# Attention units of a macaron layer: four places per unit in the projection stream in place of three, and two loads of the output projection issued earlier

## The chip, the cores and the metric

The kernel runs on all 8 NeuronCores of one Trainium2 chip. Every core works on its own rows, with no exchange between cores. The metric is the device time of the slowest core in microseconds.

## What is computed

The input has shape (4, 4096, 2048), in float32. One layer applies three residual blocks, each behind a layer norm: a feed-forward block, attention, and the same feed-forward block again.

```python
x = x + 0.5 * ffn(layernorm(x))      # relu(x W1) -> 8 softmax weights; V, U of rank 64 per weight
x = x + attn(layernorm(x))
x = x + 0.5 * ffn(layernorm(x))

# attn: 16 heads of 128; blocks of 64 tokens see the blocks at a distance of at most 2
mask = where(abs(block_i - block_j) <= 2, 0, -1e30)
scores = q @ k.T * 128 ** -0.5 + mask
out = softmax(scores) @ v            # per head, then out @ Wo
```

## The kernel before

A core computes 2048 rows of one batch entry (16 tiles of 128) and reads one tile more (17, `NT`) for the keys and values at its edge. All matmuls take bf16 operands. The program is written engine by engine: `Prog` keeps a list of instructions for each engine, `op` makes each VectorE and ScalarE instruction wait for the one before it on its own engine, and nothing is reordered later. What a helper issues first stands first in the engine's queue.

The kernel has four stages: the first feed-forward block, attention, the output projection with Wo, and the last feed-forward block. The changed lines are in the second and third.

**Attention.** The outer loop runs over 8 pairs of heads (`pr`), the inner one over 6 groups of tiles (`GROUPS`: 3, 2, 3, 3, 3, 3 tiles). For each group `proj` issues *pieces*: K for each head of the pair, Q for each head, and V for each tile. A piece is 16 matmuls into one of the four banks `R[0..3]`. K and Q pieces have as many columns as the group (384, or 256 for two tiles; the last group's Q pieces have 256, since the 17th tile has no queries), V pieces 256. ScalarE evicts K (line 675) and V (line 663), VectorE evicts Q (line 680). A pair has 41 pieces.

**Units.** A *unit* is the attention of one query tile for the two heads of a pair; a pair has 16, so there are 128. `unit` returns closures:

- `scores` (lines 763 to 780): four matmuls into the single PSUM tile `pS`, the maximum over keys on VectorE (line 770), two exponentials on ScalarE into `Praw[b]` (line 773), the reciprocal of the sums on VectorE (line 778), and two multiplications into `Pn[b]` on VectorE (line 780).
- `turn` (lines 786 to 799): six transposes of `Pn[b]` on TensorE (line 791) into the single tile `pL`, and one copy to `PTs[b]` on VectorE (line 799).
- `values` (lines 801 to 822): six PV matmuls (line 806) from `PTs[b]` into `R[4]`, a copy to `ost` on VectorE (line 814), and after a group's last unit a store of `ost` to the DRAM tensor `od` on SP's queue.

`b` alternates between two buffers. After every piece `between` issues what has been planned for this slot, in the order in which it was planned. `start_unit(k, ...)` plans `scores` at slot k, `turn` at k+3 and `values` at k+4. `next_units` starts the units that a finished group makes possible, two slots apart, from the slot after the next group's first piece; a group gives 2 or 3 units. So the units of one group run between the pieces of the next, and those of the last group between the next pair's first pieces, or, after the last pair, between the first pieces of the output projection.

**Output projection.** `wo_piece(t, cg)` issues 16 matmuls of 512 columns (line 923) for a tile and a quarter of the columns, from `Ob[g % 2]` (attention's output for a group, read back from `od`) and `Wo[cg]`; VectorE adds the result to the residual tile `Xc` (line 929). The first twelve pieces are those of tiles 0 to 2, and the last units run between them. `load_o(g)` and `load_x1(t)` are issued on SP's queue. For groups 0 and 1 they are issued once the pair loop has ended. `Ob` lies in the memory of one of the two K, V and Q buffers, which the last pair doesn't use. `load_o(2)` is issued when the pieces of tiles 0 to 2 are done. `load_w1c(0)` on POOL's queue waits for the last PV and the last stores of `ost` (`attn_end`).

Of the kernel before, what the change touches and what calls it, by code (L numbers as in the profile page):

```python
# [19 lines left out]
NQ = 16  # L20
# [6 lines left out]
QGROUPS = [(0, 3), (3, 2), (5, 3), (8, 3), (11, 3), (14, 2)]  # L27
NG = 6
GROUP_OF = {t: g for g, (a, n) in enumerate(GROUPS) for t in range(a, a + n)}
PAIRS = 8  # L30
# [111 lines left out]
def build_nc():  # L142
# [31 lines left out]
    def S(name):  # L174
        if name not in sems:
            sems[name] = Sem(ctx.enter_context(nc.semaphore(name)))
        return sems[name]
# [3 lines left out]
    def view(t, off, *dims):  # L181
        return bass.AP(t, off, [[t.ap().ap[0][0], 128], *[list(d) for d in dims]])
# [71 lines left out]
    def w_cols(dram, col0, width):  # L254
        n = dram.shape[1]
        return bass.AP(dram, col0, [[n, 128], [128 * n, 16], [1, width]])
# [487 lines left out]
    def unit(pr, t):  # L744
        s = pr % 2
        u = units[0]
        units[0] += 1
        b = u % 2
        j0 = 1 if t == 0 else 0
        c0 = j0 * 128  # L750
        w = 384 - c0
        g_k = GROUP_OF[t + 1]
        kept = {}

        def scores():
            p.wait("tensor", *[kq_end[(pr, g)] for g in range(g_k + 1)], q_end[(pr, GROUP_OF[t])],
                   S_ended[0])
            for h in range(2):
                for half in range(2):
                    lo = max(c0, 64 * half)  # L760
                    hi = 320 + 64 * half
                    key = (t - 1) * 128 + lo
                    tok = p.mm(lambda e, h=h, half=half, lo=lo, hi=hi, key=key: e.matmul(  # L763
                        pS[64 * half:64 * half + 64, h * 512 + lo: h * 512 + hi],
                        Qb[s][:, h * NQ * 128 + t * 128 + 64 * half:
                              h * NQ * 128 + t * 128 + 64 * half + 64],
                        Kb[s][:, h * NT * 128 + key: h * NT * 128 + key + hi - lo],
                        start=True, stop=True), last=(h == 1 and half == 1))
            a = att[b]
            mx = p.op("vector", lambda e: e.reduce_max(  # L770
                a[:, 0:2], view(pS, c0, (512, 2), (1, w)), AX.X, negate=True), tok)
            for h in range(2):
                ex = p.op("scalar", lambda e, h=h: e.activation(  # L773
                    Praw[b][:, h * 384 + c0:(h + 1) * 384],
                    pS[:, h * 512 + c0: h * 512 + 384], AF.Exp, bias=a[:, h:h + 1],
                    accum_out=a[:, 2 + h:3 + h]), mx, pn_free[b])
            S_ended[0] = ex
            p.op("vector", lambda e: e.reciprocal(a[:, 4:6], a[:, 2:4]), ex)  # L778
            for h in range(2):
                nm = p.op("vector", lambda e, h=h: e.tensor_scalar_mul(  # L780
                    Pn[b][:, h * 384 + c0:(h + 1) * 384],
                    Praw[b][:, h * 384 + c0:(h + 1) * 384], a[:, 4 + h:5 + h]),
                    kept.get("pt"))
            kept["nm"] = nm

        def turn():
            p.wait("tensor", kept["nm"], PT_ended[0])
            for h in range(2):
                for j in range(j0, 3):
                    o = h * 384 + j * 128  # L790
                    tok = p.mm(lambda e, o=o: e.transpose(  # L791
                        pPT[:, o:o + 128], Pn[b][:, o:o + 128], idb[:, :]),
                        last=(h == 1 and j == 2))
            pn_free[b] = tok
            if j0:
                out, src = (view(x, 128, (384, 2), (1, 256)) for x in (PTs[b], pPT))
            else:
                out, src = PTs[b][:, :], pPT[:, 0:768]
            PT_ended[0] = kept["pt"] = p.op("vector", lambda e: e.tensor_copy(out, src), tok)  # L799

        def values():
            p.wait("tensor", kept["pt"], O_ended[0], *[v_end[(pr, g)] for g in range(g_k + 1)])
            for h in range(2):
                for j in range(j0, 3):
                    o = (t - 1 + j) * 256 + h * 128
                    tok = p.mm(lambda e, h=h, j=j, o=o: e.matmul(  # L806
                        R[4][:, h * 128:(h + 1) * 128], Vb[s][:, o:o + 128],
                        PTs[b][:, (h * 3 + j) * 128:(h * 3 + j + 1) * 128],
                        start=(j == j0), stop=(j == 2)), last=(h == 1 and j == 2))
            last_unit[pr] = tok  # L810
            g = GROUP_OF[t]
            a, n = QGROUPS[g]
            o = (pr * NG + g) % 3
            O_ended[0] = p.op("vector", lambda e: e.tensor_copy(
                view(ost[o], (t - a) * 128, (n * 128, 2), (1, 128)),
                view(R[4], 0, (128, 2), (1, 128))), tok, ost_store[o])
            if t == a + n - 1:
                dst = bass.AP(od, 2 * pr * NQ * 128 + a * 128,
                              [[16 * NQ * 128, 128], [NQ * 128, 2], [1, n * 128]])
                ost_store[o] = p.dma("sync", S(f"so{o}"), dst,  # L820
                                     view(ost[o], 0, (n * 128, 2), (1, n * 128)), O_ended[0])
                ost_tok.setdefault(g, []).append(ost_store[o])

        return scores, turn, values

    def between():

# [4 lines left out]
    def plan(k, f):  # L832
        events.setdefault(k, []).append(f)

    def start_unit(k, pr, t):
        scores, turn, values = unit(pr, t)
        plan(k + 4, values)
        plan(k + 3, turn)
        plan(k, scores)

    ready_after = [(0, 2), (2, 4), (4, 7), (7, 10), (10, 13), (13, 16)]
# [10 lines left out]
    def next_units(pr, g, k):  # L852
        for i, t in enumerate(range(*ready_after[g])):
            start_unit(k + 2 * i, pr, t)
# [3 lines left out]
    def load_wo(cg, *tokens):  # L858
        wo_tok[cg] = p.dma("gpsimd", S(f"wo{cg}"), view(Wo[cg], 0, (512, 16), (1, 512)),
                           w_cols(dwo, cg * 512, 512), *tokens)  # L860

    for pr in range(PAIRS):
        for g in range(NG):
            work = [("k", 0), ("k", 1), ("q", 0), ("q", 1)]
            work += [("v", k) for k in range(GROUPS[g][1])]
            for n, (kind, k) in enumerate(work):
                proj(kind, pr, g, k)
                if pr == 0 and g == 0:
                    if n >= 4:
                        turns[n - 4]()  # L870
                    if n == 6:
                        mask_corners()
                        load_slabs(1, *[q for t in (14, 15, 16)
                                        for q in (x1_tok.get(t), ln2_apply[t])])
                        load_xn2T(5, first.v_done[NG - 1], first.w1_done[(NG - 1, 15)])
                if n == 0 and g == 0:
                    if pr == 0:
                        pass
                    elif pr < PAIRS - 1:
                        load_slabs(pr + 1, proj_done[(pr - 1, NG - 1)])  # L880
                    else:
                        load_wo(0, proj_done[(pr - 1, NG - 1)])
                between()
            next_units(pr, g, slot[0])
            if pr == PAIRS - 1 and g in (1, 2, 4):
                load_wo({1: 1, 2: 2, 4: 3}[g], proj_done[(pr, g)])


    p.stage("output")
    xs_c = Pool([])  # L890
    buf6 = proj_done[(PAIRS - 2, NG - 1)]
    end7 = proj_done[(PAIRS - 1, NG - 1)]
    xs_c.give(0, buf6)
    xs_c.give(1, proj_done[(PAIRS - 1, 4)])
    for s in (2, 3, 4, 5, 6):
        xs_c.give(s, end7)
    xc = {}
    o_tok = {}
    o_ended = [last_unit[PAIRS - 2]] * 2
    wo_done = {}  # L900

    def load_x1(t):
        s, free = xs_c.take()
        xc[t] = (s, p.dma("sync", S(f"dxc{s}"), Xc[s][:, :], x1d[t * 128:(t + 1) * 128, :],
                          x1_tok[t], *free))

    def load_o(g):
        a, n = QGROUPS[g]
        src = bass.AP(od, a * 128, [[16 * NQ * 128, 128], [NQ * 128, 16], [1, n * 128]])
        o_tok[g] = p.dma("sync", S(f"lo{g % 2}"), view(Ob[g % 2], 0, (n * 128, 16), (1, n * 128)),  # L910
                         src, o_ended[g % 2], *ost_tok[g])

    x2_add = {}
    x2_tok = {}

# [20 lines left out]
                          x2_add[t])  # L936
        xs_c.give(s, x2_tok[t])

    load_o(0)
    for t in range(0, 3):  # L940
        load_x1(t)
    load_o(1)
    for t in range(3, 5):
        load_x1(t)
    W1ctok = [None] * 8

# [216 lines left out]
```

How the kernel before makes its waits and increments, by code:

```python
                def run(e):  # L97
                    for kind, a, sem, v in lst:
                        if kind == "wait":
                            e.wait_ge(a.h, sem)
                        else:
                            ins = a(e)
                            if sem is not None:
                                ins.then_inc(sem.h, v)
```

## Time and profile before

| | |
|---|---|
| median of 3 runs | 2205.14 us (2204.86 to 2445.35) |
| profiled execution, its own time | 2203.52 us |
| its span, slowest core (core 7) | 2201.9 us |
| spans of the eight cores | 2189.0 to 2201.9 us |
| TensorE busy | 1885.9 us (86%) |
| VectorE busy | 819.0 us (37%) |
| ScalarE busy | 525.5 us (24%) |
| mean granted TensorE clock, core 7 | 0.953 |
| attention stage, about | 590 to 1543 us of the span |
| output projection, about | 1552 to 1788 us |

All rows are of one execution, and where no core is named, of core 7. Busy time of TensorE includes the modelled tail of a matmul. An idle time stands with the instruction that ended it and with the engine and line that it had waited for. A granted clock of 1.00 is 2.4 GHz; the other level is 0.50, and a value between them is a mean over a stretch.

### The profile page before, as it was taken

Reading aid. Unit: us, or ns where it says so; the run is one execution under the profiler, and the core shown is the slowest. Engines: PE = TensorE matmul, PEld = TensorE weight load, DVE = VectorE, ACT = ScalarE, POOL = GpSimd, SP = SyncE. Lnnn points to the kernel's source line nnn. Section 1 sums busy time; section 2 is a strip of 40 time slices with the busy share of each in tenths; the row PEclk is TensorE's granted clock in tenths of the full one; section 3 lists DMA queues with packets and bytes.
Section 4 is the critical chain, followed back from the end, with each engine's and each line's share of the span. In section 5 each row is a group of like instructions: output and inputs, shape, how many; then the busy total and the mean of one; then the engine's idle time right before and its main releaser. Section 6 shows DMA issues by size and latency. Waiting matters only on the chain.

```text
span 2201.9 us, 35898 instructions; the slowest of 8 cores (2189.0 to 2201.9 us)
## 1 busy us (share of the span) xinstructions
PE 1885.9 (86%) x13876; PEld 1197.6 (54%) x13876; DVE 819.0 (37%) x1509; ACT 525.5 (24%) x1121; POOL 47.0 (2%) x46
## 2 busy tenths in 40 slices
PE   3966786868888989989898999998889969998998
PEld 2743443435566666666666666666334437555554
DVE  4055242433434444444444444444311142224322
ACT  2222322222222222222222222222000012232221
POOL 1000000000000000000000000000000000000000
PEclk9988897989999999999999999999999979999999
DMA  9912213217662305050505032155496880122211
GB/s 191 172 60 87 77 58 86 87 58 160 163 115 31 45 11 68 7 68 11 68 7 70 10 45 34 24 78 81 161 258 198 209 135 1 58 77 115 96 58 58
DMA packets 145033, 186.94 MB, mean 85 GB/s; under 512 B 3680, under 2 KB 132704, under 8 KB 133728
## 3 DMA queue, kind: packets, MB, share of 16 engines
q0 software_dynamic: 81696, 58.76, 20.4%
q1 hardware_dynamic: 62736, 125.84, 17.3%
q8 instruction: 112, 1.84, 0.3%
q14 instruction: 57, 0.47, 0.1%
q10 hardware_dynamic: 432, 0.05, 0.0%
HBM read 180.99 MB, written 62.39 MB: 111 GB/s over the span
## 4 chain that ended last, share of the span: by engine, by line
PE 58%; DVE 20%; ACT 8%; DMA 7%; issue 5%; DVEq 1%; SPq 0%; ACTq 0%; POOLq 0%
PE R L352 18%; PE R L669 13%; PE R L923 9%; ACT Praw L773 6%; PE R L439 5%; PE R L407 5%; DVE lnb L296 4%; DVE att L770 4%; DVE Pn L780 4%; DMA Xa<-x 3%; PE R L658 3%; DVE PTs L799 2%; DVE Qb L680 2%; PE R L806 2%; DMA Ob<-od 2%
## 5 line engine op out<-in xcount | busy, mean ns | idle before, releaser
L658 PE MATMUL R<-wvS,xn2T 128*128 128x256 bf16 x2176 | 266.7, 277 | 4.1 <-ACT Kb L675 4.1
L352 PE MATMUL R<-xnTa,W1a 128*128 128x384 bf16 (+1 forms) x1536 | 261.5, 330 | 5.4 <-ACT xnTa L323 5.4
L669 PE MATMUL R<-xn2T,wkS 128*128 128x384 bf16 (+1 forms) x1536 | 252.9, 318 | 0.0
L352 PE MATMUL R<-xnTc,W1c 128*128 128x384 bf16 (+1 forms) x1536 | 238.4, 314 | 3.5 <-ACT xnTc L323 3.5
L923 PE MATMUL R<-Wo,Ob 128*128 128x512 bf16 x1024 | 227.3, 384 | 14.6 <-DMA Ob<-od 14.6
L669 PE MATMUL R<-xn2T,wqS 128*128 128x384 bf16 (+1 forms) x1536 | 238.3, 309 | 0.0
L773 ACT ACTIVATE Praw<-pS,att 128x384 f32<-128x384 f32 (+1 forms) x256 | 147.3, 575 | 377.1 <-DVE att L770 364.9
L658 PEld LDWEIGHTS R<-wvS,xn2T 128*128 128x128 bf16 x2176 | 208.8, 99 | 36.6 <-issue 12.3
L352 PEld LDWEIGHTS R<-xnTa,W1a 128*128 128x128 bf16 x1536 | 148.9, 101 | 92.2 <-issue 22.0
L669 PEld LDWEIGHTS R<-xn2T,wkS 128*128 128x128 bf16 x1536 | 144.9, 98 | 87.3 <-issue 12.2
L669 PEld LDWEIGHTS R<-xn2T,wqS 128*128 128x128 bf16 x1536 | 145.2, 98 | 77.2 <-issue 11.8
L352 PEld LDWEIGHTS R<-xnTc,W1c 128*128 128x128 bf16 x1536 | 146.5, 99 | 72.8 <-issue 8.8
L923 PEld LDWEIGHTS R<-Wo,Ob 128*128 128x128 bf16 x1024 | 100.6, 99 | 137.6 <-issue 22.0
L806 PE MATMUL R<-PTs,Vb 128*128 128x128 bf16 x752 | 62.6, 218 | 97.0 <-DVE PTs L799 97.0
L296 DVE BATCH_NORM_STATS2 lnb<-Xa 128x6 f32<-128x512 f32 x136 | 94.4, 694 | 113.6 <-DMA Xa<-x 99.6
L770 DVE TENSOR_REDUCE att<-pS 128x2 f32<-128x768 f32 (+1 forms) x128 | 120.4, 941 | 42.0 <-PE pS L763 20.8
L780 DVE TENSOR_SCALAR Pn<-Praw,att 128x384 bf16<-128x384 f32 (+1 forms) x256 | 106.4, 416 | 27.6 <-DVE att L778 0.3
L806 PEld LDWEIGHTS R<-PTs,Vb 128*128 128x128 bf16 x752 | 47.5, 97 | 121.4 <-issue 116.1
L929 DVE TENSOR_TENSOR Xc<-Xc,R 128x512 f32<-128x512 f32 x64 | 44.0, 688 | 183.3 <-PE R L923 182.8
L799 DVE COPY PTs<-pL 128x768 bf16<-128x768 bf16 (+1 forms) x128 | 70.3, 549 | 109.6 <-PE pL L791 95.5
L778 DVE RECIPROCAL att<-att 128x2 f32<-128x2 f32 x128 | 21.2, 166 | 210.0 <-ACT Praw L773 210.0
L359 ACT ACTIVATE hTc<-R,b1T 128x384 bf16<-128x384 f32 (+1 forms) x96 | 52.5, 547 | 194.6 <-PE pL L373 174.2
(73 smaller groups left out, 1516.0 us busy)
## 6 DMA issues: line engine op xcount, KB each, us to landing
Xa<-x SPq DMA_DIRECT2D x17, 1024.0 KB, 13.3
x1d<-Xa SPq DMA_DIRECT2D x16, 1024.0 KB, 4.0
Xc<-x1d SPq DMA_DIRECT2D x16, 1024.0 KB, 15.1
y<-Xc SPq DMA_DIRECT2D x16, 1024.0 KB, 4.0
x2d<-Xc SPq DMA_DIRECT2D x11, 1024.0 KB, 6.2
Xc<-x2d SPq DMA_DIRECT2D x11, 1024.0 KB, 10.2
wkS<-wk POOLq DMA_DIRECT2D x8, 1024.0 KB, 12.8
wqS<-wq POOLq DMA_DIRECT2D x8, 1024.0 KB, 20.0
```

Of the source, the lines that this page charges most:

```text
L296: p.op("vector", lambda e, i=i, j=j, x=x: e.bn_stats(st[:, i * 24 + j * 6: i * 24 + j * 6 + 6], x[:, j * 512:(j + 1) * 512]), tokens[i])
L352: tok = p.mm(lambda en, c=c: en.matmul(bank[:, 0:w], slot[:, c * 512 + (e % 4) * 128: c * 512 + (e % 4 + 1) * 128], xnT[:, c * w:(c + 1) * ...
L407: tok = p.mm(lambda e, c=c: e.matmul(bank[:, :], xnT[:, c * w + t * 128: c * w + (t + 1) * 128], self.V[:, c * 512:(c + 1) * 512], start=( ...
L439: done = p.mm(lambda e, kc=kc, bank=bank, cg=cg: e.matmul(bank[:, :], zT[:, kc * 128:(kc + 1) * 128], self.U[:, kc * D + cg * 512: kc * D ...
L658: tok = p.mm(lambda e, c=c: e.matmul(bank[:, 0:256], xn2T[g][:, c * src_w + k * 128: c * src_w + (k + 1) * 128], wvS[s][:, c * 256:(c + 1) ...
L669: tok = p.mm(lambda e, c=c: e.matmul(bank[:, 0:w], wS[:, c * 256 + k * 128: c * 256 + (k + 1) * 128], xn2T[g][:, c * src_w: c * src_w + w] ...
L770: mx = p.op("vector", lambda e: e.reduce_max(a[:, 0:2], view(pS, c0, (512, 2), (1, w)), AX.X, negate=True), tok)
L773: ex = p.op("scalar", lambda e, h=h: e.activation(Praw[b][:, h * 384 + c0:(h + 1) * 384], pS[:, h * 512 + c0: h * 512 + 384], AF.Exp, bias ...
L780: nm = p.op("vector", lambda e, h=h: e.tensor_scalar_mul(Pn[b][:, h * 384 + c0:(h + 1) * 384], Praw[b][:, h * 384 + c0:(h + 1) * 384], a[: ...
L799: PT_ended[0] = kept["pt"] = p.op("vector", lambda e: e.tensor_copy(out, src), tok)
L806: tok = p.mm(lambda e, h=h, j=j, o=o: e.matmul(R[4][:, h * 128:(h + 1) * 128], Vb[s][:, o:o + 128], PTs[b][:, (h * 3 + j) * 128:(h * 3 + j ...
L923: tok = p.mm(lambda e, h=h: e.matmul(bank[:, :], Ob[g % 2][:, h * w + (t - a) * 128: h * w + (t - a + 1) * 128], Wo[cg][:, h * 512:(h + 1) ...
```

## The change

The normalisation (reciprocal and two multiplications) is taken out of `scores` into a closure of its own, `weights`, planned one slot after the scores. `turn` stays at k+3. `values` goes from k+4 to k+5. The wait for `pn_free[b]` (the transposes of the unit that had the buffer before) goes from the exponentials to the multiplications. `load_o(0)` and `load_x1(0)` are issued in the last pair 6 slots after group 1's last piece (slot 19 of 41, `early_o`), and `load_o(1)` 6 slots after group 2's (slot 26), in place of once the pair loop has ended. The helpers `load_x1` and `load_o` move up in the file, otherwise unchanged.

```diff
@@ unit
-                    accum_out=a[:, 2 + h:3 + h]), mx, pn_free[b])
-            S_ended[0] = ex
-            p.op("vector", lambda e: e.reciprocal(a[:, 4:6], a[:, 2:4]), ex)
+                    accum_out=a[:, 2 + h:3 + h]), mx)
+            S_ended[0] = kept["ex"] = ex
+
+        def weights():
+            p.op("vector", lambda e: e.reciprocal(a[:, 4:6], a[:, 2:4]), kept["ex"])
             for h in range(2):
-                nm = p.op("vector", lambda e, h=h: e.tensor_scalar_mul(
+                kept["nm"] = p.op("vector", lambda e, h=h: e.tensor_scalar_mul(
                     Pn[b][:, h * 384 + c0:(h + 1) * 384],
-                    Praw[b][:, h * 384 + c0:(h + 1) * 384], a[:, 4 + h:5 + h]),
-                    kept.get("pt"))
-            kept["nm"] = nm
+                    Praw[b][:, h * 384 + c0:(h + 1) * 384], a[:, 4 + h:5 + h]), pn_free[b])
...
@@ start_unit
-        scores, turn, values = unit(pr, t)
-        plan(k + 4, values)
+        scores, weights, turn, values = unit(pr, t)
+        plan(k + 5, values)
         plan(k + 3, turn)
+        plan(k + 1, weights)
         plan(k, scores)
...
@@ before the pair loop
+    def early_o():
+        o_ended[0] = o_ended[1] = last_unit[PAIRS - 2]
+        load_o(0)
+        xs_c.give(0, proj_done[(PAIRS - 2, NG - 1)])
+        load_x1(0)
...
@@ the pair loop
             next_units(pr, g, slot[0])
+            if pr == PAIRS - 1 and g == 1:
+                plan(slot[0] + 6, early_o)
+            if pr == PAIRS - 1 and g == 2:
+                plan(slot[0] + 6, lambda: load_o(1))
...
@@ output
-    o_ended = [last_unit[PAIRS - 2]] * 2
...
-    load_o(0)
-    for t in range(0, 3):
-        load_x1(t)
-    load_o(1)
-    for t in range(3, 5):
+    for t in range(1, 5):
         load_x1(t)
```

## Rows read from the trace of the kernel before

**Rows 1.** The page: its span, and each engine's busy time in us.

```profile
span 2201.9 us, 35898 instructions; the slowest of 8 cores (2189.0 to 2201.9 us)
...
PE 1885.9 (86%) x13876; PEld 1197.6 (54%) x13876; DVE 819.0 (37%) x1509; ACT 525.5 (24%) x1121; POOL 47.0 (2%) x46
```

**Rows 2.** Waits of TensorE: line, releaser, us in total, times, longest.

```profile
PE R L806 <- DVE PTs L799: 97.0, 76, 2.7
...
PE R L923 <- DMA Ob<-od: 14.6, 2, 9.1
```

**Rows 3.** Timeline, TensorE: start us, us, instructions merged, in brackets the idle time before.

```profile
1010.79 1.91 PE L658 MATMUL R<-wvS,xn2T 128*128 128x256 bf16 x16
1013.78 0.49 PE L806 MATMUL R<-PTs,Vb 128*128 128x128 bf16 x6 [1.08 <-DVE PTs L799]
...
1014.60 1.92 PE L658 MATMUL R<-wvS,xn2T 128*128 128x256 bf16 x16
1016.35 0.50 PE L791 MATMUL pL<-idb,Pn 128*128 128x128 bf16 x6
...
1019.99 2.76 PE L669 MATMUL R<-xn2T,wkS 128*128 128x384 bf16 x16
1022.59 0.50 PE L791 MATMUL pL<-idb,Pn 128*128 128x128 bf16 x6
```

**Rows 4.** Busy time of stretches, here two pair periods: length, engines, clock, DMA.

```profile
977.21:1096.63 119.42, 106.99 (x908) 75.67 (x909) 52.74 (x108) 33.22 (x93) 3.44 (x3) 1.00 0.26 36
...
1336.60:1456.47 119.87, 108.50 (x908) 76.73 (x909) 52.74 (x108) 33.22 (x93) 1.15 (x1) 0.99 0.15 28
```

**Rows 5.** Timeline, VectorE and TensorE around one late copy.

```profile
1036.58 0.96 DVE L770 TENSOR_REDUCE att<-pS 128x2 f32<-128x768 f32 x1 [0.17 <-DVE ost L814]
...
1037.96 0.50 PE L791 MATMUL pL<-idb,Pn 128*128 128x128 bf16 x6
...
1039.18 0.17 DVE L778 RECIPROCAL att<-att 128x2 f32<-128x2 f32 x1 [1.64 <-ACT Praw L773]
...
1039.45 0.95 DVE L780 TENSOR_SCALAR Pn<-Praw,att 128x384 bf16<-128x384 f32 x2
...
1040.57 0.56 DVE L799 COPY PTs<-pL 128x768 bf16<-128x768 bf16 x1 [0.17 <-DVE Pn L780]
...
1041.27 0.49 PE L806 MATMUL R<-PTs,Vb 128*128 128x128 bf16 x6 [1.06 <-DVE PTs L799]
```

**Rows 6.** Groups by line and shape, 977.21 to 1096.63: VectorE's evictions (busy, mean ns).

```profile
L814 DVE CAST ost<-R 128x256 bf16<-128x256 f32 x16 | 6.8, 424 | 12.4 <-PE R L806 11.7 <-DVE Pn L780 0.7
L680 DVE TENSOR_SCALAR Qb<-R 128x384 bf16<-128x384 f32 x8 | 4.5, 557 | 5.3 <-PE R L669 4.6 <-DVE Pn L780 0.7
...
L680 DVE TENSOR_SCALAR Qb<-R 128x256 bf16<-128x256 f32 x4 | 1.7, 424 | 0.7 <-DVE Pn L780 0.3 <-DVE ost L814 0.2 <-PE pS L763 0.2
```

**Rows 7.** Timeline, TensorE, at the start of the output projection.

```profile
1552.41 5.60 PE L923 MATMUL R<-Wo,Ob 128*128 128x512 bf16 x16 [9.10 <-DMA Ob<-od]
1557.85 0.50 PE L791 MATMUL pL<-idb,Pn 128*128 128x128 bf16 x6
...
1558.67 3.63 PE L923 MATMUL R<-Wo,Ob 128*128 128x512 bf16 x16
1562.13 0.50 PE L806 MATMUL R<-PTs,Vb 128*128 128x128 bf16 x6
```

**Rows 8.** A stretch at that place: behind POOL's column are clock, DMA share, GB/s.

```profile
1550.00:1555.00 5.00, 2.59 (x7) 0.94 (x8) 0.00 (x0) 0.00 (x0) 0.00 (x0) 0.50 1.00 350
```

**Rows 9.** Chain of waits and POOL's timeline: issue us, us (loads: to landing).

```profile
1539.24 13.04 DMA Ob<-od
...
1601.87 31.21 DMA Ob<-od
...
1593.90 1.14 POOL L91 DMA_DIRECT2D W1c<-w  x1 [70.97 <-PE R L923]
```

**Rows 10.** A stretch of the output projection, columns as in rows 4.

```profile
1640.00:1785.00 145.00, 145.00 (x674) 65.73 (x673) 28.92 (x43) 0.00 (x0) 3.42 (x3) 1.00 0.75 196
```

More of the change, by code:

```diff
@@ L752, in unit @@
         g_k = GROUP_OF[t + 1]
+        a = att[b]
         kept = {}
@@ L768, in scores @@
                         start=True, stop=True), last=(h == 1 and half == 1))
-            a = att[b]
             mx = p.op("vector", lambda e: e.reduce_max(
@@ L822, in values @@
                 ost_tok.setdefault(g, []).append(ost_store[o])
-        return scores, turn, values
+        return scores, weights, turn, values
     def between():
@@ L860, in load_wo, with load_x1, load_o @@
                            w_cols(dwo, cg * 512, 512), *tokens)
+    xs_c = Pool([])
+    xc = {}
+    o_tok = {}
+    o_ended = [None, None]
+    wo_done = {}
+    def load_x1(t):
+        s, free = xs_c.take()
+        xc[t] = (s, p.dma("sync", S(f"dxc{s}"), Xc[s][:, :], x1d[t * 128:(t + 1) * 128, :],
+                          x1_tok[t], *free))
+    def load_o(g):
+        a, n = QGROUPS[g]
+        src = bass.AP(od, a * 128, [[16 * NQ * 128, 128], [NQ * 128, 16], [1, n * 128]])
+        o_tok[g] = p.dma("sync", S(f"lo{g % 2}"), view(Ob[g % 2], 0, (n * 128, 16), (1, n * 128)),
+                         src, o_ended[g % 2], *ost_tok[g])
+    def early_o():
[3 more added lines that the diff above has]
+        load_x1(0)
     for pr in range(PAIRS):
@@ L889, in build_nc @@
     p.stage("output")
-    xs_c = Pool([])
-    buf6 = proj_done[(PAIRS - 2, NG - 1)]
     end7 = proj_done[(PAIRS - 1, NG - 1)]
-    xs_c.give(0, buf6)
     xs_c.give(1, proj_done[(PAIRS - 1, 4)])
@@ L896, in build_nc @@
         xs_c.give(s, end7)
-    xc = {}
-    o_tok = {}
-    o_ended = [last_unit[PAIRS - 2]] * 2
[L900 to L911, printed above, removed]
     x2_add = {}
```

## The prediction

> **What bounds the kernel now.** I first read the head of the page: the slowest core spans 2201.9 us and TensorE is busy for 1885.9 of them; the next engine, VectorE, for 819.0 [rows 1]. So only what makes TensorE stand, or slows its clock, is worth anything. The waits of TensorE say what makes it stand: 97.0 us in 76 waits of the PV matmuls (line 806) for VectorE's copy of the transposed weights (line 799), and 14.6 us in two waits of the output projection for Ob [rows 2].
>
> Then I read one stretch of TensorE's timeline, where the pattern of the attention stage shows. A piece (16 matmuls of a projection) of 256 columns takes 1.75 us from its start to the next item (1014.60 to 1016.35), one of 384 columns 2.60. After the first V piece (1010.79) the PV matmuls start at 1013.78, which is 2.99 us later in place of 1.75 [rows 3]. So that wait costs 1.24 us where the view counts 1.08: it takes the last matmul's modelled tail of some 0.16 us as work. One pair of heads shows it whole: 119.42 us, 106.99 of them busy, 12.43 idle [rows 4]; ten such waits end in it, so TensorE needs some 107.0 - 10 x 0.16 = 105.4 us for a pair.
>
> Why is the copy late? VectorE's rows answer: after the scores come the reduction (start 1036.58), then 1.64 us of standing until both exponentials are through on ScalarE, then the reciprocal (1039.18), the two multiplications into Pn (1039.45, 0.95 us) and only then the copy to PTs (1040.57), though its transposes ended at 1038.46. PV starts 0.14 us after the copy ends [rows 5]. Reduction to end of multiplications is one block of 3.82 us in a strict queue, and the next unit's copy stands behind it, with one 1.75 us piece as TensorE's only cover.
>
> **The change, part by part.** No instruction is added or removed in the units: the same 128 units issue the same matmuls and VectorE operations. They are only placed otherwise. Three edits answer together.
>
> (a) reciprocal and multiplications are issued one piece after the scores. Between reduction and reciprocal VectorE now takes the next piece's Q eviction (0.56 or 0.42 us, [rows 6]) instead of standing. (b) PV comes two pieces after its transposes, not one. (c) pn_free is awaited by the multiplication in place of the exponential. TensorE passed it three pieces ago; cost nothing.
>
> Work the new order out for a seven-piece group (K K Q Q V V V), units A, B, C started after pieces 1, 3, 5: after piece 1 PV of B', transposes of C', scores of A; after 2 weights of A; after 3 PV of C', scores of B; after 4 transposes of A, weights of B; after 5 scores of C; after 6 PV of A, transposes of B, weights of C; PV of B falls after piece 1 of the next group. The shortest cover of a copy is now V+V, 3.5 us, plus the scores' 0.4. The copy needs transposes 0.50, 0.11 to start, 0.56, 0.14 to PV: 1.31 us if VectorE is free, and what can stand before it is one Q eviction or one PV eviction (0.42), no longer a whole block. So the wait is gone for all 76.
>
> The new order could only move the wait. The places with least room, laid out with the durations of rows 5 and 6 from the end of the group's first K piece: in the group of two tiles (six pieces of 1.75) B's reduction runs 6.5 to 7.4, behind a Q and a PV eviction; its reciprocal starts 2.60 after that start, at 9.1, its multiplications end at 10.3; its transposes come at 11.05. Room 0.6 us. In the last group, whose Q pieces have 256 columns, C's scores need the PSUM that B's exponentials read: these end 9.6, the scores come at 10.2. Room 0.5. Everywhere else there is over 1 us. I take 1 us in all for small misses; the bounds are 0, and one miss of the present size, 1.8 to 2.1 us less its room, in each of 8 pairs, 12 us.
>
> Gain of the attention stage: 97.0 + 76 x 0.16 = 109.2 us (taking the same tail for all 76). Bounds: 97.0 (if the tails do not come back) and 109.2.
>
> TensorE's clock: in the attention of this core three pairs have a short time at the lower level. One of them is the second row of its group: 119.87 us at a mean of 0.99, in place of 119.42 at 1.00 [rows 4]. Without stands I take these away too, 3 x 0.45 = 1.3 us; bounds 0 and 1.3.
>
> (d) In the output stage Ob's first load and the first x1 tile are issued 19 pieces into the last pair, Ob's second load after 26. Each keeps its condition (all eight stores of its group), and the groups' last PVs come after 18 and 25 pieces, so SP stops only until the store before has landed, with its next store six pieces off. They pass the stores of groups 2 and 3 on SP's queue; POOL's Wo loads share the engines, but are wanted 15 or more pieces later. Today Ob's load is issued at 1539.24 and lands 13.04 us later [rows 9]. TensorE stands 9.10 us, with the tail 9.26. After that stand the granted clock is at its lower level (0.50 from 1550 to 1555). The first piece then takes 5.44 us instead of the 3.46 of the next one [rows 7, 8]. The gain is 9.26 + 1.98 = 11.2 us on this core. The x1 tiles 1 to 4 are still issued around the end of the projections; tile 1 is first wanted after the second output piece, 6.9 us in, tile 2 3.5 us later, and no Ob load is in front of them now, so I cost them nothing.
>
> What is late next: Ob's third load. It waits for the last use of the first buffer, is issued at 1601.87 and lands 31.21 us later [rows 9], which makes the other 5.5 us of line 923's 14.6. The change doesn't move it. But W1c's load, on POOL, waits for the last PV (1593.90 today), and that now comes one output piece later, 3.46 + 0.33 = 3.8 us nearer. W1c then begins its 2 MB before the Ob load by 4 us rather than 8, and stays longer beside it. I take +2 us, with bounds 0 and 3.8.
>
> **Sum**, against the profiled execution: 2201.9 - 109.2 - 1.3 - 11.2 + 1 + 2 = 2083.2 us of span. That run's own time is 1.6 us above its span (2203.52), and the median of the runs 1.6 above that (2205.14). So 2086.
>
> **The rule that speaks against it.** Without gaps TensorE would work the attention stage at nearly its full rate on eight cores. Does the clock allow it? From 1640 to 1785 this core runs the output projection without a gap, 145.00 us busy of 145.00, at a granted clock of 1.00, which is 2.4 GHz, while the others do the same work [rows 10]. The Trainium skill (TensorE: Matmul & The Clock Gate, Part 1, "Seeing it yourself") warns that a peak-current limit takes a die to 13/16 of the clock once three of its cores run dense matmuls. By that rule the attention's 844 us would become some 1039, an estimate from that page, and the kernel some 2281 us. The trace disagrees with it for 145 us.
>
> **Rivals.** *The clock falls (slower).* Its place is the attention stage, 8 x 105.4 = 844 us of TensorE work. The change saves 120 us in all, so it decides from a mean granted clock of 844 / 964 = 0.875 down. With half of the time at each level (mean 0.75) the stage takes 281 us more: 2367 us. The page named above would bring it. For it: the clock does fall here at times [rows 4, 8]; against it: it falls beside stands, and the dense stretch has 1.00 [rows 10]. Chance 0.03.
>
> *The wait moves to another place in VectorE's queue.* The transposes or scores meet late multiplications or exponentials, since the chain of 3.82 us is still serial. With one miss of today's 1.23 in each of six groups of each pair it keeps 59 us: 2145 us. For it: two places with half a microsecond of room. Against: VectorE works only 52.74 of 119.42 us [rows 4]. Chance 0.09.
>
> *The output's gain is given back.* Ob's third load lands later by what the projection starts earlier on all cores together, or x1 comes late: 2086 + 11 = 2097. For it: the DMA engines there are full already, share 1.00 [rows 8]. Chance 0.09.
>
> *Nothing comes of it* (the copy wasn't what PV waited for, and another engine stands in): 2200. All 76 waits name the copy, and rows 5 show PV starting right behind it. Chance 0.02.
>
> **How the numbers follow.** My forecast has 0.77. Its own range: 2074 (no misses, and the 5.5 us wait and its share of slow clock gone) to 2113 (tails not regained 12, misses 12, 2 more at Ob). The 8-in-10 range takes in the output rival and a little towards the moved wait: 2070 to 2118. Faster by over 2% (below 2161; 2% is about what a measurement of this kernel can tell) holds for forecast, moved wait and output: 0.95. Same 0.02, slower 0.03.
>
> **What would show it.** Right: PV's waits for line 799 near 0 in place of 97.0; a pair period near 105.5; the first output matmul right behind the last V piece at full clock; Ob's third load still awaited. Wrong: new waits of line 791 on the multiplications or of 763 on the exponentials (the margins fail); a granted clock under 1.00 in the middle of attention; waits of line 923 adding up to 14 us or more.

## The result, and the profile after

The changed kernel took 2097.35 us (median of 4 runs, 2079.8 to 2128.0), and its time is 0.9485 of that of the kernel before (95% interval 0.9329 to 0.9641). In some executions of both kernels one die, or two cores of one, ran at a lower clock for a while (2445.35 us, twice, before; 2128.0 us and the profiled 2107.71 us after), and the times called undisturbed below leave all of these out, while the ratios keep most of those with only two cores. Undisturbed, the median is 2081.9 us for the changed kernel (nine runs over three comparisons, 2076.7 to 2089.7) and 2205.0 us for the one before (23 runs), a ratio of 0.944. The forecast was 2086, with a range of 2070 to 2118, so the measured median lies 11 us above the forecast and inside the range.

The profiled execution took 2107.71 us, and its slowest core is not one on which the change shows undisturbed. These are the spans of the cores:

```profile
core 0: 2073.5 us, clock 0.957
...
core 2: 2102.9 us, clock 0.942
core 3: 2106.2 us, clock 0.942
...
core 7: 2069.4 us, clock 0.957
```

Cores 2 and 3 are 30 us behind the others at a lower mean clock. So I read core 7 here, the one that was read before, and come back to core 3. Waits on core 7, for rows 2, the first one of VectorE and the others of TensorE:

```profile
DVE att L780 <- ACT Praw L773: 68.9, 54, 2.7
...
PE pS L277 <- DVE xnc L310: 15.2, 1, 15.2
...
PE R L933 <- DMA Ob<-od: 4.7, 2, 3.1
PE R L658 <- ACT Kb L675: 4.1, 1, 4.1
```

The 97 us of line 806 are gone on every core, and nothing of lines 764 (scores) or 791 (transposes) has come in their place but the 1.5 us for the mask that were there before. The output projection (line 933, 923 before) waits 4.7 us for Ob in place of 14.6. One period of a pair of heads, columns as in [rows 4]:

```profile
927.00:1032.39 105.39, 105.39 (x910) 76.36 (x908) 52.72 (x108) 33.12 (x93) 3.44 (x3) 1.00 0.28 41
```

TensorE is busy in all of 105.39 us, where it was 119.42 us with 12.4 idle [rows 4]. The queue of VectorE, for [rows 5], with TensorE's rows between (timeline, core 7):

```profile
976.41 0.50 PE L791 MATMUL pL<-idb,Pn 128*128 128x128 bf16 x6
976.68 0.56 DVE L680 TENSOR_SCALAR Qb<-R 128x384 bf16<-128x384 f32 x1 [1.15 <-PE R L669]
...
977.41 0.56 DVE L799 COPY PTs<-pL 128x768 bf16<-128x768 bf16 x1 [0.17 <-DVE Qb L680]
978.14 0.17 DVE L780 RECIPROCAL att<-att 128x2 f32<-128x2 f32 x1 [0.17 <-DVE PTs L799]
978.41 0.94 DVE L782 TENSOR_SCALAR Pn<-Praw,att 128x384 bf16<-128x384 f32 x2
...
979.53 0.96 DVE L770 TENSOR_REDUCE att<-pS 128x2 f32<-128x768 f32 x1 [0.17 <-DVE Pn L782]
...
980.74 0.50 PE L806 MATMUL R<-PTs,Vb 128*128 128x128 bf16 x6
```

The copy (977.41) now stands ahead of the reciprocal (978.14), and here the reciprocal finds its exponentials done: it starts 0.17 us behind its neighbour where it stood 1.64 us. Not every one does. VectorE still stands for the exponentials in 54 units, 68.9 us in all, where it stood in all 128, 210.0 us; but no PV matmul waits behind it any more. The copy ends at 977.97 and PV comes at 980.74. The end of the attention stage, for [rows 7]:

```profile
1420.43 1.91 PE L658 MATMUL R<-wvS,xn2T 128*128 128x256 bf16 x16
1422.18 3.62 PE L933 MATMUL R<-Wo,Ob 128*128 128x512 bf16 x16
1425.63 0.50 PE L806 MATMUL R<-PTs,Vb 128*128 128x128 bf16 x6
```

The first output piece follows the last V piece after 1.75 us, with no stand, and takes 3.45 us at full clock. The table shows where core 7's time went, from the first and last starts of the V and output matmuls:

| core 7, us | before | after | difference |
|---|---|---|---|
| up to the first V piece | 591.9 | 587.8 | -4.1 |
| first to last V matmul | 949.6 | 834.3 | -115.3 |
| last V matmul to first output matmul | 10.9 | 0.1 | -10.8 |
| first to last output matmul | 235.1 | 232.0 | -3.1 |
| from there to the end | 414.4 | 415.2 | +0.8 |
| span | 2201.9 | 2069.4 | -132.5 |

The first row isn't the change's: no changed line runs ahead of the first V piece.

Now core 3 of the same profile, in two stretches of dense work behind the output projection's last Ob wait (busy time of stretches; clock, DMA share and GB/s stand last):

```profile
1615.00:1675.00 60.00, 60.00 (x231) 24.82 (x229) 9.63 (x14) 0.00 (x0) 2.28 (x2) 0.81 0.77 106
1705.00:1770.00 65.00, 62.99 (x457) 43.30 (x456) 15.02 (x22) 16.32 (x28) 0.00 (x0) 0.81 0.01 2
```

And core 7 at the same work:

```profile
1598.00:1655.00 57.00, 56.53 (x262) 25.45 (x260) 11.35 (x17) 0.00 (x0) 3.42 (x3) 1.00 0.77 138
1705.00:1770.00 65.00, 64.28 (x500) 43.76 (x499) 6.66 (x13) 16.11 (x30) 0.00 (x0) 1.00 0.00 1
```

Core 3 runs 60 us without a gap at a granted clock of 0.81, so it gets 231 matmuls of 512 columns through in 60 us where core 7 gets 262 through in 57. From 600 us on to the end of the attention stage all eight cores were at 1.00. Core 2 shows the same level in the same stretches. The level begins at 1612 and ends at 1773 of the span, with the stand between two stages in it, so some 136 us of work lie at it. They cost about 136 x 0.19 = 26 us, an estimate from these rows.

### The profile page after: what moved, and what is told of

It is laid out like the page before. It is cut to its first block, busy times and chain, and to the rows that moved or that the text cites. A ratio compares the mean times of both kernels' runs of the same rounds, so it can differ in the third digit from the quotient of the medians.

```text
span 2106.2 us, 35974 instructions; the slowest of 8 cores (2056.7 to 2106.2 us)
## 1 busy us (share of the span) xinstructions
PE 1889.6 (90%) x13876; PEld 1204.4 (57%) x13876; DVE 819.2 (39%) x1509; ACT 524.8 (25%) x1121; POOL 47.0 (2%) x46
## 4 chain that ended last, share of the span: by engine, by line
PE 81%; DMA 7%; DVE 6%; ACT 3%; issue 1%; SPq 0%; DVEq 0%; ACTq 0%; POOLq 0%
PE R L669 22%; PE R L352 20%; PE R L658 12%; PE R L933 9%; PE R L439 5%; PE R L407 5%; DVE lnb L296 4%; DMA Xa<-x 3%; PE pS L764 2%; DMA Ob<-od 2%; PE pL L791 2%; PE R L806 2%; PE pS L277 2%; DMA W1a<-w 1%; DMA Xc<-x2d 1%
## 5 line engine op out<-in xcount | busy, mean ns | idle before, releaser
L658 PE MATMUL R<-wvS,xn2T 128*128 128x256 bf16 x2176 | 259.0, 274 | 4.1 <-ACT Kb L675 4.1
L352 PE MATMUL R<-xnTc,W1c 128*128 128x384 bf16 (+1 forms) x1536 | 248.2, 323 | 3.4 <-ACT xnTc L323 3.4
L933 PE MATMUL R<-Wo,Ob 128*128 128x512 bf16 x1024 | 238.3, 398 | 9.3 <-DMA Ob<-od 9.3
L658 PEld LDWEIGHTS R<-wvS,xn2T 128*128 128x128 bf16 x2176 | 207.5, 98 | 34.7 <-issue 12.2
L814 DVE CAST ost<-R 128x256 bf16<-128x256 f32 x128 | 54.4, 425 | 170.8 <-PE R L806 160.5
L373 PE MATMUL pL<-W2b,hTa 128*128 128x8 bf16 x272 | 20.7, 167 | 84.4 <-ACT hTa L359 82.0
```

What stands on the lines that cost most here:

```text
L352: tok = p.mm(lambda en, c=c: en.matmul(bank[:, 0:w], slot[:, c * 512 + (e % 4) * 128: c * 512 + (e % 4 + 1) * 128], xnT[:, c * w:(c + 1) * ...
L658: tok = p.mm(lambda e, c=c: e.matmul(bank[:, 0:256], xn2T[g][:, c * src_w + k * 128: c * src_w + (k + 1) * 128], wvS[s][:, c * 256:(c + 1) ...
L814: O_ended[0] = p.op("vector", lambda e: e.tensor_copy(view(ost[o], (t - a) * 128, (n * 128, 2), (1, 128)), view(R[4], 0, (128, 2), (1, 128 ...
L933: tok = p.mm(lambda e, h=h: e.matmul(bank[:, :], Ob[g % 2][:, h * w + (t - a) * 128: h * w + (t - a + 1) * 128], Wo[cg][:, h * 512:(h + 1) ...
```

## The experiments

Theory A says that the placing of the units takes all PV waits away and the early loads give up to 11 us; A1, that either of the two edits of a unit would do alone. Theory B ties the level of 0.81 to the gapless attention. The third edit of a unit, the wait for `pn_free` at the multiplications, is in every variant. Times are from undisturbed runs; intervals are those of the ratios to the kernel before in the same comparison.

**The changed kernel once more**, beside the next three.

> The changed kernel once more, beside the others. Theory A (the placement of the units gives nearly all, some 109 us of attention; the early loads give up to 11 us on the cores that stood longest): 2080 to 2090 us where no core shows a granted clock of 0.81, and 15 to 30 us more where a die does. Theory B (the third clock level belongs to the gapless attention): the granted clock would be below 1.00 inside the attention stage, between 590 and 1480 us of the span; theory A expects 1.00 there and the 0.81 only in the output projection or behind it.

2076.7, 2083.9 and 2089.7 us, ratio 0.9425 (0.9349 to 0.9501). No core of its profile shows another level than 0.50 and 1.00. In the same comparison a run of the kernel *before* had cores 2 and 3 at mean clocks of 0.944 and 0.941, and took 2225.2 us, where its neighbours took 2202.7 to 2209.7. Theory B expected the level inside the attention stage; neither trace of the changed kernel shows it there, and the kernel before, whose attention has gaps, has a pair of cores with the same low mean. So theory B falls in its form. Whether denser work brings the level more often stays open.

**Order of the units alone**, loads as before:

```diff
-            if pr == PAIRS - 1 and g == 1:
-                plan(slot[0] + 6, early_o)
-            if pr == PAIRS - 1 and g == 2:
-                plan(slot[0] + 6, lambda: load_o(1))
...
-    for t in range(1, 5):
+    o_ended[0] = o_ended[1] = last_unit[PAIRS - 2]
+    load_o(0)
+    for t in range(0, 3):
+        load_x1(t)
+    load_o(1)
+    for t in range(3, 5):
         load_x1(t)
```

> The units as changed (normalisation one piece after the scores, PV two pieces after the transposes), but the first two Ob loads and the first x1 tile issued after the pair loop, as before. Theory A: PV waits for the copy stay at 0, TensorE waits 4 to 12 us for the first Ob load again on every core, time about 2086 + 8 to 11 = 2094 to 2097 us. Rival (the early loads are hidden anyway, their gain is given back at the third Ob load): as the changed kernel, within 3 us.

2092.5, 2097.7 and 2105.5 us (and 2114.5 with cores 6 and 7 at mean clocks of 0.94), ratio 0.9512 (0.9436 to 0.9588). No PV wait. The first Ob wait is back, and longer than in the kernel before (core 3, timeline):

```profile
1434.93 5.78 PE L930 MATMUL R<-Wo,Ob 128*128 128x512 bf16 x16 [14.22 <-DMA Ob<-od]
```

On the eight cores this first Ob wait is 7.3 to 14.9 us. Without the early loads the kernel is 14 us slower than with them in this comparison (2097.7 to 2083.9, medians of three), where I expected 8 to 11; the three runs of this variant lie 13 us apart, so the excess isn't shown. Nor is all of it the first wait: on core 3 the third and the sixth load of Ob are awaited too, 8.9 and 6.8 us. The rival (their gain is given back) falls.

**Early loads alone**, units as before (`plan(k, weights)` right behind the scores, `plan(k + 4, values)`).

> The units as before (normalisation right behind the scores, PV one piece after the transposes); the first two Ob loads and the first x1 tile issued early as in the changed kernel. Theory A: the 97 us of PV waits stay, the first Ob wait is gone on every core, and the time falls by 8 to 13 us to 2193 to 2199 us. Rival (the loads' gain is given back at the third Ob load): 2203 to 2209 us, as before.

2190.0 to 2200.8 us in ten runs, median 2195.8, ratio 0.9954 (0.9927 to 0.9982): 9 us, inside what was expected. The first Ob wait is gone on all eight cores. The waits, on core 6:

```profile
PE R L806 <- DVE PTs L799: 97.7, 77, 2.7
...
PE R L933 <- DMA Ob<-od: 9.5, 2, 4.9
```

All of PV's waits stay. This variant has the new place of the `pn_free` wait with the old order, so that edit by itself takes no PV wait away. The two halves add up to 9 us for the loads and 107 for the order (2205.0 to 2097.7), together 116 of the 123 measured; the 7 us between are less than the spread of the runs with the order alone.

**PV two pieces after the transposes, but no split:**

```diff
-        plan(k + 1, weights)
         plan(k, scores)
+        plan(k, weights)
```

> Of the two edits of the unit only one: PV two pieces after the transposes, the normalisation right behind the scores as before; early loads as changed. Theory A1 (either edit alone takes the wait away, since the copy is ready 2.83 us after the transposes today and the shortest cover is then 3.5 us): PV waits of 0 to 5 us in all, time within 5 us of the changed kernel. Rival A2 (only both edits together do it): half of the 97 us of waits stays, about 2135 us.

2096.0, 2098.5 and 2100.3 us, ratio 0.9492 (0.9424 to 0.9561). Both theories missed: the waits are 10.5 to 10.6 us in 19, on each core, and from the first to the last V matmul it takes 849 us on core 3, against 834. That is 14.9 us for 10.6 + 19 x 0.16 = 13.6 us. The waits view of core 3:

```profile
PE R L806 <- DVE PTs L799: 10.6, 19, 1.0
```

Eight of the 19, 5.8 us, stand where the pieces are short. VectorE's timeline on core 3, in a group of two tiles:

```profile
933.16 0.96 DVE L770 TENSOR_REDUCE att<-pS 128x2 f32<-128x768 f32 x1 [0.17 <-DVE ost L814]
935.75 0.17 DVE L780 RECIPROCAL att<-att 128x2 f32<-128x2 f32 x1 [1.63 <-ACT Praw L773]
936.03 0.95 DVE L782 TENSOR_SCALAR Pn<-Praw,att 128x384 bf16<-128x384 f32 x2
937.15 0.42 DVE L680 TENSOR_SCALAR Qb<-R 128x256 bf16<-128x256 f32 x1 [0.17 <-DVE Pn L782]
937.75 0.42 DVE L799 COPY PTs<-pL 128x512 bf16<-128x512 bf16 x1 [0.17 <-PE R L658]
```

And TensorE's there, the transposes of that unit and its PV:

```profile
933.79 0.39 PE L791 MATMUL pL<-idb,Pn 128*128 128x128 bf16 x4
938.32 0.38 PE L806 MATMUL R<-PTs,Vb 128*128 128x128 bf16 x4 [0.65 <-DVE PTs L799]
```

In the group of two tiles the block from reduction to multiplications (933.16 to 936.98) and a Q eviction run past even two pieces. I had taken the copy's lateness from a V piece of a long group (2.83 us behind its transposes) and not from this place, where the kernel before shows its waits of 2.07 us. Four more waits, 0.73 to 0.83 us, stand behind two multiplications that took 1.34 to 1.64 us in place of 0.95, and the other seven are of 0.24 us.

**The split, but PV one piece after the transposes** (`plan(k + 4, values)`).

> Of the two edits of the unit only the other one: the normalisation one piece after the scores, PV one piece after the transposes as before; early loads as changed. Theory A1: the copy then stands directly behind the transposes, 1.31 us with VectorE free against a cover of 1.75 us, so PV waits stay under 10 us and the time is within 10 us of the changed kernel. Rival A2: half of the 97 us of waits stays, about 2135 us. Rival A3 (the cover matters and the split does not): 97 us of waits stay, about 2190 us.

2080.5, 2081.1 and 2081.5 us (and 2107.5 with cores 4 and 5 at mean clocks of 0.94), ratio 0.9454 (0.9344 to 0.9563). No core has a PV wait. VectorE and TensorE on core 3:

```profile
984.85 0.50 PE L791 MATMUL pL<-idb,Pn 128*128 128x128 bf16 x6
...
985.46 0.56 DVE L799 COPY PTs<-pL 128x768 bf16<-128x768 bf16 x1 [0.58 <-PE pL L791]
...
986.51 0.17 DVE L780 RECIPROCAL att<-att 128x2 f32<-128x2 f32 x1 [0.49 <-ACT Praw L773]
...
986.93 0.50 PE L806 MATMUL R<-PTs,Vb 128*128 128x128 bf16 x6
```

The copy starts 0.11 us behind its transposes, ends at 986.02, and one V piece (1.75 us) covers it. So the split takes all of the wait away by itself, and the second piece between transposes and PV is slack. Of theory A1 this half holds and the other, PV later alone, does not. Cause and cover can be told apart here: take the block from in front of the copy and one piece is enough; leave it there and two are not.

**Ob's third load first**, to find what is left in the output projection:

```diff
+    load_o(2)
-    load_w1c(0, *attn_end)
+    load_w1c(0, *attn_end, o_tok[2])
     for t in range(3):
         store_x2(t)
```

> The changed kernel with Ob's third load issued ahead of the first three x2 stores, and W1c's first load held until that Ob load has landed. Theory C (the third Ob load is late because W1c's load and three x2 stores share its time): the wait ahead of tile 5, 1.5 to 6 us on each core, goes to 0, and with it the stretch at the lower clock behind it; 4 to 8 us faster than the changed kernel, about 2072 to 2080 us. Rival D (the load is bound by its own 1.5 MB in small rows with eight cores loading at once): the wait stays over 2 us and the time as it is.

The wait ahead of tile 5 is gone on all eight cores: theory C holds for it. W1c's load is issued when Ob's has landed, so the two issues tell how long Ob's took (core 7, queues of SP and POOL):

```profile
1457.18 0.52 SPq L91 DMA_DIRECT2D Ob<-od  x1
1457.75 2.70 SPq L91 DMA_DIRECT2D x2d<-Xc  x3
...
1466.08 1.14 POOL L91 DMA_DIRECT2D W1c<-w  x1 [70.99 <-DMA Ob<-od]
```

That is at most 8.9 us from issue to landing (8.8 to 12.1 on the eight cores), where core 7 of the changed kernel has 27.2. The wait ahead of tile 14 stays on five cores, 2.4 to 6.3 us. The time is inconclusive, 2078.1 us in the one undisturbed run and 2099.1 in the profiled one, whose cores 0 and 1 ran at 0.81 from 1604 on (core 0):

```profile
1605.00:1668.00 63.00, 61.58 (x235) 25.32 (x233) 10.83 (x16) 0.00 (x0) 3.54 (x4) 0.81 0.76 100
```

**More cover for Ob's sixth load:** six pieces of tiles 11 to 13 ahead of the first of tile 14.

```diff
     for cg in range(4):
-        for t in range(last, NQ):
-            wo_piece(t, cg)
+        if cg == 0:
+            for c, t in [(0, 11), (0, 12), (0, 13), (1, 11), (1, 12), (1, 13), (0, 14), (0, 15)]:
+                wo_piece(t, c)
+        elif cg == 1:
+            for t in (14, 15):
+                wo_piece(t, 1)
+        else:
+            for t in range(last, NQ):
+                wo_piece(t, cg)
```

> The changed kernel with only the order of eight pieces of the last group changed: six pieces of tiles 11 to 13 (two column quarters) stand ahead of the first piece of tile 14, in place of three. Ob's sixth load (issued when tile 10 is done) then has 20.8 us of cover and not 10.4. Theory C: the wait ahead of tile 14, about 3 to 6 us on the cores that have it, goes; 3 to 6 us faster on those cores, 2075 to 2084 us for the slowest. Rival D: the wait stays, since the load lands later than 20.8 us after its issue.

2073.7, 2074.2 and 2077.8 us, ratio 0.9404 (0.9343 to 0.9465). The wait ahead of tile 14 is gone on all cores; that ahead of tile 5 stays on seven, 1.4 to 6.3 us. No changed kernel ran in this comparison, so how much of the time this edit gives alone isn't shown.

**Both Ob edits.**

> Both edits of the two kernels before. Theory C: no wait of the output projection for Ob on any core, TensorE gapless from the first score to the last output piece, about 2066 to 2074 us. Rival D: at least one of the two waits stays; 2076 us or more.

2070.8 us (median of five undisturbed runs, 2069.2 to 2073.1), ratio 0.9384 (0.934 to 0.9428). In its profile no core waits for Ob, and from the middle of attention's first pair to the last output matmul no core's granted clock falls. It beats both kernels, so I ran it again beside the changed kernel and beside the form with the split alone.

> The changed kernel beside the two below, on the same chip. 2076 to 2090 us.

2080.4 to 2084.8 us in four runs (and 2111.5 with cores 6 and 7 at mean clocks of 0.94), ratio 0.9464 (0.9413 to 0.9515).

> The split of the normalisation alone (PV one piece after the transposes), with both Ob edits. Theory A1 (the split alone takes all PV waits away, the second piece of cover is slack): 0 us of PV waits and 0 of Ob, 2067 to 2074 us, the same as the kernel with PV two pieces later within 2 us. Rival: small waits of PV come back beside other traffic, 2078 us or more.

2067.6 to 2072.5 us in four runs, ratio 0.938 (0.9362 to 0.9397). No wait for PTs or Ob on any core.

> The changed kernel with both Ob edits once more: 2067 to 2074 us, 8 to 15 us below the changed kernel of the same call.

2067.7 to 2073.6 us in five runs, ratio 0.9386 (0.9369 to 0.9404). By their medians (2069.0 and 2071.3) the two forms are some 2 us apart, with intervals that overlap, as it should be where the second piece of cover is slack. Both are 10 to 13 us under the changed kernel of the same comparison (2081.8).

## Why the prediction was right or wrong

**The steps that failed.** The cause of the PV wait was read rightly, and the undisturbed time is 4 us from the forecast. Three steps failed. The largest is TensorE's clock: the sum put nothing for it in the output projection and the last stage, because one execution had held 1.00 for 145 us of the output projection. In the profiled execution two cores worked 136 us at 0.81, which cost some 26 us, and the median of the four runs, 2097.35, is the middle between that execution (2107.71) and one without (2086.98). The second is the attention term, 109.5 us in the sum and 116.5 in the trace. The third is that the sum gave the PV wait to two edits together: the split alone leaves no wait, the longer cover alone leaves 10.6 us.

**The attention stage: mechanism right, term 7 us too small.** The pair period was worked out as 105.4 us and is 105.39. The sum took 76 waits of the waits view, 109.2, and 1.3 for the clock, less 1 us for misses: 109.5; the stage gave 115.3 on core 7 up to the last V matmul, and the last of the 76 waits, 1.2 us, ended behind it: 116.5. The step that was off was to price the stage from the count of waits and not from the periods: (119.42 - 105.39) x 8 is 112.2 already, and the kernel before shows a wait of 2.69 us in its first pair with slow clock behind it besides. No miss came at the two narrow places: TensorE waits neither for the multiplications nor, but for the mask, for `pS`. In the group of two tiles the multiplications were worked out to end 0.6 us ahead of the transposes' start, with the hand-over; they do so by 0.64 (core 7):

```profile
1030.90 0.94 DVE L782 TENSOR_SCALAR Pn<-Praw,att 128x384 bf16<-128x384 f32 x2
```

with the transposes at 1032.62.

**Three edits that "answer together".** This was true of the sum and wrong as an explanation. The prediction gave the wait to two causes, the block ahead of the copy and the single piece of cover, and priced them as one. The split alone does it; the second piece alone leaves 10.6 us of waits, 15 us of the stage.

**The output's first wait: right on core 7** (11.2 worked out; of the 10.8 us in the table 1.2 is the last PV wait and 0.3 PV itself, and the first piece takes 3.45 us as forecast), and for the slowest core of a run 9 us alone and 14 us on top of the new order. It was read on one core. Before, the first waits for Ob were 3.7 to 12.2 us on cores 0 to 7, so what the early loads take away differs by core.

**What is late next: the right load, the term of 2 us not shown.** Ob's third load was to come 2 us later, since W1c's load moves nearer to it. W1c is indeed issued closer (1464.98, 5.0 us ahead of Ob's load, where it was 8.0), but the load lands earlier, 27.23 us after its issue in place of 31.21 [rows 9], and the wait is 1.54 us in place of 5.5. That is core 7 alone. On cores 1 to 3 the wait grew, and over the eight cores its mean was 3.5 us before and 2.8 and 3.7 us in the two profiles of the changed kernel: neither the +2 us of the sum nor a gain is shown. The chain of waits of core 7, Ob's third and sixth load from issue to landing:

```profile
1469.98 27.23 DMA Ob<-od
...
1581.78 11.95 DMA Ob<-od
```

TensorE's timeline at the two waits that remain:

```profile
1497.46 2.75 PE L933 MATMUL R<-Wo,Ob 128*128 128x512 bf16 x12 [1.54 <-DMA Ob<-od]
...
1593.98 6.38 PE L933 MATMUL R<-Wo,Ob 128*128 128x512 bf16 x21 [3.12 <-DMA Ob<-od]
```

The experiment with that load first shows that the sharing makes the wait (landing after 8.9 us in place of 27.2). W1c's hold and the stores' place were changed together, though the stores still follow only 0.6 us behind Ob's load there, so which of the two weighs more is open. And there is a second late load that the prediction did not see, Ob's sixth. It is issued when tile 10 is done and wanted three pieces (10.4 us) later, and takes 11.95 us. Cores 1, 3, 4 and 6 had that wait before (2.1 to 4.6 us), core 7 had not; in the changed kernel's profile six cores have it (3.1 to 7.7 us). Reading one core's waits hid it.

**The clock: rival wrong in place, right in kind.** The forecast gave 0.03 to a fall of the clock, in the attention stage, and took the 145 us at 1.00 [rows 10] as the answer to the rule of the page. The attention stage ran at 1.00 on all eight cores from 600 us on. But in the profiled execution two cores ran 136 us at 0.81 in the output projection and the last stage, and this alone puts its 2107.71 us 22 us above the forecast. That page (the Trainium skill, TensorE: Matmul & The Clock Gate, Part 1, "Seeing it yourself") gives 13/16 = 0.8125 for this level, and the trace agrees with the value. It does not agree with the condition in the executions that were traced: eight cores ran dense for 820 us at 1.00, and the level came to one pair of cores and not to their whole die. The failing step was to infer from one undisturbed execution that a level doesn't exist. The kernel before has pairs of cores with the same low mean clock (2225.2 us, where its neighbours took 2202.7 to 2209.7), so the level isn't shown to be an effect of the change.

**Rivals.** The wait did not move within VectorE's queue, the output's gain was not given back, and something came of it. The sum was 121.7 us of gains less 1 and less 2, so 119; measured between undisturbed runs it is 2205.0 - 2081.9 = 123 us. That these are so near is in part luck. The sum was for core 7's span, 2083.2 us, and core 7 came to 2069.4: of the 13.8 us, 7.0 are the attention term, 3.5 the output projection, and 4.1 stand ahead of the attention stage, with 0.8 the other way behind it. The slowest core of an undisturbed run is one that waits longer for Ob: 2075.2 us on core 2 in the repeated profile, with 8.9 us of such waits.

## What to carry to other kernels

When an engine stands between two instructions of one unit in a strict queue, what is queued behind pays for it: issue the second half a piece later and the next unit's work moves in front. It cost nothing here. Price a repeated stage by its period less the work in it, and not by adding up the waits, which leave out each one's tail. Read the waits of all cores before saying which load is late next, since a load that one core just meets stalls its neighbour.

## What the runs showed of the hardware

A third clock level of 0.81 came to a pair of cores (2 and 3; in another kernel 0 and 1), from 1612 to 1773 and from 1604 to 1763 of the span, on both cores of the pair at the same time, while no other core showed it. In both it lasted some 160 us, across a stand between two stages in which the clock was at 0.50 and from which it came back to 0.81. It began in dense output matmuls some 8 us after the last Ob wait, and not in every execution; the kernel before and other variants have pairs of cores (0 and 1, 2 and 3, 4 and 5, 6 and 7) with a mean near 0.94. Two multiplications of VectorE took 1.34 to 1.64 us in place of 0.95 at four places of the variant without the split (core 3), and at each POOL was issuing a load of weights meanwhile:

```profile
904.90 1.54 DVE L782 TENSOR_SCALAR Pn<-Praw,att 128x384 bf16<-128x384 f32 x2
905.14 1.15 POOL L91 DMA_DIRECT2D wkS<-wk  x1 [103.55 <-PE R L658]
```

The cause wasn't tried.
